# GpSimd's low halves signalled piece by piece, weights kept earlier, the second PV behind K's projection, and a split wait for the first scores, in a banded attention and FFN kernel

## The chip, the core and the metric

The kernel runs on one core of one Trainium2 chip. The metric is the device time of one execution in microseconds. The kernel before took 2201.57 us (median of 3 runs, 2192.87 to 2208.58 us).

## What is computed

For 8 batches of 1024 rows by 512, the reference computes a layer norm, 16 heads of attention in which scores outside a band of 64 columns to either side are set to 0 (and still count in the softmax), and a small network of 64 units with 16 hidden values each. Input, attention and network are added:

```python
xn = layernorm(x)
Q, K, V = (xn @ W + b for (W, b) in ((Wq, bq), (Wk, bk), (Wv, bv)))    # 16 heads of 64
columns = where(band, Q @ K.T, 0.0)
out = softmax(columns) @ V @ Wo + bo
s = xn @ Win + bin_
g = sum(relu(s[..., None] * W1 + b1) * W2) + b2
return x + out + (g @ Wout + bout)
```

## The kernel before

**Steps.** Two heads make a pair, so there are 8 pairs in each of 8 batches, and the program of each engine is one call of `run_steps` (L187) that issues 66 steps. Step n has k = n modulo 8. It projects Q, K and V for pair n (`project`, L1133, matmuls on L1143), it attends for pair j = n - 1 (scores, softmax), and it weighs the values (`weigh_values`, L1188, matmuls on L1199) and projects the output (`project_out`, L1149, L1158) for pair o = n - 2. The network's parts are hung into certain steps: k = 0 its input, k = 1 to 4 the 16 hidden values (on DVE L906), k = 5 its split and the next batch's statistics, k = 6 and 7 its output (L1180). The order of work on each engine is written out by hand in its `step` function, and the engines meet through counted semaphores.

**Split numbers.** Each factor is held as a high and a low half, and a product is three passes of matmuls: hi*hi, hi*lo, lo*hi. So each tile has a high half that ACT writes (a rounding copy) and a low half that DVE or GpSimd (POOL) writes as the difference.

**Softmax of pair j.** PE writes scores of two 128-row tiles and both heads per call (`scores(tp)`, tp 0 to 3, L1121, 12 matmul pairs). DVE scales and masks them into `probs` and takes the row maxima (`mask_scores`, L842 to L861), ACT exponentiates (L532), DVE makes the denominators of one half of the rows in four small instructions (`denominators(half)`: L866 `row_l`, L869, L871, L873 `neg_e`), POOL normalises eight 128x256 tiles of that half (`normalise_weights`, L388, each instruction increments `normed`), ACT rounds four of them into `p_hi` (L588), and POOL writes the low half of four tiles, `p_lo` (`weights_low(half, h)`, L399 to L403). In a step POOL runs output_low(0), normalise(0), low(0,0), output_low(1), normalise(1), low(0,1), low(1,0), low(1,1). Of the four instructions of one `weights_low` only the last increments the semaphore `p_lo`:

```python
for t in tiles_of(half):
    last = pool.tensor_tensor(p_split[lo][:, h, t], probs[:, h, t], p_split[hi][:, h, t], ALU.subtract)
last.then_inc(p_lo, 1)
```

SyncE (SP) then transposes the weights by DMA, one DMA for each half, head and part (`transpose_weights`, L240 to L247), and PE's `weigh_values(half)` waits for the four transposes of its half. In the text PV(0) and PV(1) are its two calls in a step.

**Values.** V's projection goes through ACT (`value_lines`, L559 to L571) into `vT`. DVE sums three partial sums into a mean in small instructions (`centre_values`: L935, L937, L939 on 128x1, then L941 subtracts it from `vT`), PE transposes `vT` at the end of the step (`transpose_values`, L1182, L1186), ACT and DVE split it, and DVE makes `v_back` (L1051, 128x1). The first DVE work of the next step is `mask_scores(0)`.

**Scores and their inputs.** ACT (L580) and DVE (`qk_low`, L930) split Q and K by halves of 512 rows, in the order Q first half, K first half, Q second half, K second half; the counter `qk_lo` rises by one for each, so by four in a step. `scores(0)`, the first work of PE in a step, waits for all four of the step before.

**Weights.** In the first 8 steps (`split`) the raw weights of pair n + 1 are split by ACT (`split_high`, L475) and DVE (L794) into the single buffer `w_split`; before ACT may overwrite it, the split of pair n must have been stored to the internal tensor `w_kept` (`keep_weights`, L217 to L219). SP issues these stores between the transposes of the step, each followed by a load of the raw weights of pair n + 2. All later steps load the kept weights (`load_kept`, L221).

Of the kernel before, what the change touches and what calls it, by code (L numbers as in the profile page):

```python
# [15 lines left out]
def band_attention_ffn(nc, x, Wq, bq, Wk, bk, Wv, bv, Wo, bo, Win, bin_, W1, b1, W2, b2, Wout, bout, out):  # L16
# [16 lines left out]
    with ExitStack() as ctx:  # L33
# [148 lines left out]
        def tiles_of(half):  # L182
            return range(4 * half, 4 * half + 4)
# [29 lines left out]
        def _(sp):  # L213
# [26 lines left out]
            def transpose_weights(j, half, h, part):  # L240
                u = 2 * half + h
                if 2 * j - 1 + half > 0:
                    sp.wait_ge(pv_done, 2 * j - 1 + half)
                sp.wait_ge((p_hi, p_lo)[part], 4 * j + u + 1)
                sp.dma_start_transpose(pT[half][h][part][:],
                                       p_split[part][:, h, 4 * half:4 * half + 4].rearrange("p t w -> p (t w)")) \
                    .then_inc(pT_in[half], 16)  # L247
# [35 lines left out]
            def step(n, b, k, proj=True, attend=True, out_proj=True, split=False, split_next=False, last=False):  # L283
                j = n - 1
                next_pair = (k + 1) % PAIRS
                loads_next = proj and not (last and k == PAIRS - 1)

                def next_weights(i):
                    if split:
                        keep_weights(n, i, k)  # L290
                        if k < PAIRS - 2:
                            load_raw(i, k + 2)
                    elif loads_next:
                        load_kept(n, i, next_pair)

                def first_kept(i):
                    sp.wait_ge(w_got[i], 16 * (n + 1))
                    load_kept(n, i, 0)

                if 2 <= n <= PAIRS + 1:  # L300
                    keep_output(n - 1, n - 2)
                elif out_proj:
                    load_output_kept(n - 1, (k - 2) % PAIRS)
                if split and k > 0:
                    load_output_raw(k)
                if k == 2 and b > 0:
                    store(b - 1, 1)
                if k in (2, 3) and not last:
                    load_x(b + 1, k - 2)
                if attend:  # L310
                    transpose_weights(j, 0, 0, hi)
                    transpose_weights(j, 0, 0, lo)
                    transpose_weights(j, 0, 1, hi)
                if k == 1 and b > 0 and proj:
                    store(b - 1, 0)
                if proj:
                    next_weights(V_)
                if attend:
                    transpose_weights(j, 1, 0, hi)
                    transpose_weights(j, 0, 1, lo)  # L320
                if proj:
                    next_weights(Q_)
                if attend:
                    transpose_weights(j, 1, 1, hi)
                if proj:
                    next_weights(K_)
                if n == PAIRS - 1:
                    first_kept(V_)
                    first_kept(Q_)
                if attend:  # L330
                    transpose_weights(j, 1, 0, lo)
                    transpose_weights(j, 1, 1, lo)
                if n == PAIRS - 1:
                    first_kept(K_)
# [12 lines left out]
        def _(pool):  # L347
# [31 lines left out]
            def step(n, b, k, proj=True, attend=True, out_proj=True, last=False, **_):  # L379
# [17 lines left out]

                def weights_low(half, h):
                    pool.wait_ge(p_hi, 4 * j + 2 * half + h + 1)  # L399
                    for t in tiles_of(half):  # L400
                        last = pool.tensor_tensor(p_split[lo][:, h, t], probs[:, h, t], p_split[hi][:, h, t],  # L401
                                                  ALU.subtract)
                    last.then_inc(p_lo, 1)  # L403

                def add_biases(p):

# [299 lines left out]
        def _(dve):  # L706
# [132 lines left out]
            def step(n, b, k, proj=True, attend=True, out_proj=True, split_next=False, last=False, **_):  # L839
                j, o = n - 1, n - 2  # L840

                def mask_scores(tp):  # L842
                    if n == 1 and tp == 0:
                        dve.wait_ge(mask_set, 1)
                    if j > 0 and tp % 2 == 0:
                        dve.wait_ge(p_lo, 4 * j - 2 + tp)
                    if j < PAIRS and tp == 0:
                        dve.wait_ge(unit_s_ready, 2 * j + 2)
                    dve.wait_ge(scored, 4 * j + tp + 1)
                    for h in range(2):  # L850
                        for i in range(2):
                            c, t = column(tp, h, i), 2 * tp + i

                            dve.tensor_tensor_reduce(out=probs[:, h, t],  # L854
                                                     in0=ps[SCORE_BANK[tp][h]][:, i * WIN:i * WIN + WIN],
                                                     in1=mask[:], scale=unit_s[:, j % PAIRS:j % PAIRS + 1],
                                                     scalar=0.0, op0=ALU.mult, op1=ALU.max,
                                                     accum_out=row_max[:, c:c + 1]).then_inc(masked, 1)
                    dve.wait_ge(masked, 16 * j + 4 * tp + 4)
                    cols = slice(4 * tp, 4 * tp + 4)  # L860
                    dve.tensor_scalar(neg_max[:, cols], row_max[:, cols], -1.0, None, ALU.mult).then_inc(max_ready, 1)  # L861
# [206 lines left out]
        def _(pe):  # L1068
# [48 lines left out]
            def step(n, b, k, proj=True, attend=True, out_proj=True, split=False, last=False, **_):  # L1117
# [2 lines left out]

                def scores(tp):  # L1121
                    if tp == 0:
                        pe.wait_ge(qk_lo, 4 * j + 4)
                    for i in range(2):
                        t = 2 * tp + i
                        for a, (qp, kp) in enumerate(PASSES):
                            for h in range(2):
                                rows = slice(h * D, h * D + D)
                                last = pe.matmul(ps[SCORE_BANK[tp][h]][:, i * WIN:i * WIN + WIN],  # L1129
                                                 qT[qp][rows, t * P:t * P + P], kT[kp][rows, t * P:t * P + WIN],  # L1130
                                                 start=(a == 0), stop=(a == 2))
                    last.then_inc(scored, 1)
# [85 lines left out]

                if attend:
                    earlier_outputs_added(5)  # L1220
                    scores(0)
                    scores(1)
                if out_proj:
# [9 lines left out]
                if attend:  # L1233
                    masks_read(0)
                    earlier_outputs_added(7)
                    scores(2)
                    scores(3)
                if out_proj:
                    if attend:
                        masks_read(1)  # L1240
                    else:
                        pe.wait_ge(o_summed, 2 * o)
                    weigh_values(1)
                if proj:
                    if attend:
                        masks_read(1)
                    project_qk(1)
                if proj and k == 0:
                    if attend:
                        masks_read(2)  # L1250
# [164 lines left out]
```

## Time and profile before

| | us |
|---|---|
| median of 3 runs | 2201.57 |
| lowest, highest | 2192.87, 2208.58 |
| the profiled execution | 2183.65 |
| its span, first to last instruction | 2181.9 |

Engines are PE (matmul), PEld (its weight loads), DVE, ACT, POOL and SP (queue). Busy time of an engine counts executing instructions, including the time that an instruction takes longer because something holds it up inside. "Idle before" in brackets names how long the engine had nothing and which instruction released it. PEclk is the granted clock of TensorE as a share of full speed, with two levels, 1.0 (2.4 GHz) and 0.5 (1.2 GHz).

### The profile page before, as it was taken

How to read it: one execution, taken by the hardware profiler on the slowest of the kernel's cores; microseconds unless marked ns; L12 is line 12 of the kernel's file. 1: busy time of each engine (PE TensorE's matmuls, PEld its weight loads, DVE VectorE, ACT ScalarE, POOL GpSimd, SP SyncE). 2: the span in 40 equal slices, each digit the busy share in tenths (PEclk: the TensorE clock that was granted, in tenths of full speed). 3: DMA queues.
4: the chain of work that ended last, by engine and by line, in shares of the span. 5: the costliest groups of instructions: out<-in, count | busy, mean ns of one | idle time of the engine just before them, and what ended most of it. 6: DMA issues, size and time to landing. Idle time of an engine off the chain costs nothing.

```text
span 2181.9 us, 42699 instructions
## 1 busy us (share of the span) xinstructions
PE 1958.2 (90%) x14211; PEld 1107.1 (51%) x14211; DVE 1824.1 (84%) x4579; ACT 1480.3 (68%) x3961; POOL 1517.1 (70%) x2272
## 2 busy tenths in 40 slices
PE   8768799998999989998899998998989998999985
PEld 4435455554555545554455554554555554555543
DVE  7779687898789887998889888889888898888775
ACT  5767667775767756766667775775757775777753
POOL 3655657877588757867578775686748876687764
PEclk8988899999999999999999999999999999999997
DMA  4454453755366543754356654375444755365534
GB/s 124 118 134 98 97 116 84 174 112 112 69 128 160 101 93 83 164 123 99 81 103 150 136 101 102 80 186 107 87 93 103 173 102 108 78 141 112 117 78 106
DMA packets 610427, 247.04 MB, mean 113 GB/s; under 512 B 547336, under 2 KB 559648, under 8 KB 610208
## 3 DMA queue, kind: packets, MB, share of 16 engines
q1 hardware_dynamic: 610160, 244.30, 50.9%
q8 instruction: 114, 1.87, 0.4%
q14 instruction: 105, 0.86, 0.1%
q10 hardware_dynamic: 48, 0.01, 0.0%
HBM read 84.84 MB, written 25.17 MB: 50 GB/s over the span
## 4 chain that ended last, share of the span: by engine, by line
PE 34%; DVE 26%; POOL 15%; ACT 13%; issue 7%; DMA 5%; SPq 1%; DVEq 0%; ACTq 0%; POOLq 0%
PE ps L1143 17%; POOL probs L388 8%; ACT probs L532 7%; POOL p_lo L401 6%; DVE acc L888 5%; PE ps L1199 5%; PE ps L1158 4%; DVE probs L854 4%; PE ps L1129 4%; DVE v_mean L935 3%; DMA pT_lo<-p_lo 3%; DVE row_l L866 3%; DVE xn L906 2%; ACT p_hi L588 2%; DMA w_kept<-w_split 1%
## 5 line engine op out<-in xcount | busy, mean ns | idle before, releaser
L1143 PE MATMUL ps<-xT_hi,w_split 128*128 128x512 f16 x3072 | 976.8, 382 | 7.9 <-issue 4.4
L388 POOL TENSOR_SCALAR probs<-probs,inv_l,neg_e 128x256 f32<-128x256 f32 x1024 | 589.9, 592 | 283.0 <-DVE neg_e L873 281.5
L401 POOL TENSOR_TENSOR p_lo<-probs,p_hi 128x256 f16<-128x256 f32 x1024 | 678.2, 697 | 39.9 <-ACT p_hi L588 39.9
L1143 PE MATMUL ps<-xT_lo,w_split 128*128 128x512 f16 x1536 | 587.0, 382 | 0.0
L532 ACT ACTIVATE probs<-probs,neg_max 128x256 f32<-128x256 f32 x1024 | 505.7, 498 | 24.4 <-DVE neg_max L861 24.2
L1143 PEld LDWEIGHTS ps<-xT_hi,w_split 128*128 128x128 f16 x3072 | 301.8, 98 | 380.0 <-issue 26.0
L854 DVE CUSTOM_DVE_ANT_0 probs<-ps,mask,unit_s 128x256 f32<-128x256 f32 x1024 | 433.2, 478 | 44.1 <-PE ps L1129 43.6
L888 DVE SCALAR_TENSOR_TENSOR acc<-ps,unit_o,acc 128x512 f32<-128x512 f32 x512 | 356.4, 740 | 30.4 <-PE ps L1158 30.4
L395 POOL TENSOR_TENSOR oT_lo<-o_sum,oT_hi 128x512 f16<-128x512 f32 x128 | 149.0, 1164 | 311.4 <-ACT o_sum L600 311.4
L1158 PE MATMUL ps<-wo_split,oT_hi 128*128 128x512 f16 x1024 | 317.9, 393 | 17.2 <-DVE xT_lo L743 9.2
L588 ACT ACTIVATE p_hi<-probs 128x1024 f16<-128x1024 f32 x256 | 269.5, 1053 | 83.1 <-POOL probs L388 82.8
L1199 PE MATMUL ps<-pT_hi,v 128*64 128x256 f16 (+1 forms) x2560 | 201.8, 260 | 47.5 <-DMA pT_lo<-p_lo 38.8
L1143 PEld LDWEIGHTS ps<-xT_lo,w_split 128*128 128x128 f16 x1536 | 151.1, 98 | 161.4 <-issue 3.3
L1129 PE MATMUL ps<-kT_hi,qT_hi 64*128 64x256 f32 x1024 | 164.7, 310 | 54.5 <-DVE kT_lo L930 46.9
L596 ACT ACTIVATE oT_hi<-ps,v_back 128x512 f16<-128x512 f32 x128 | 86.7, 677 | 168.7 <-PE ps L1199 168.7
L1158 PE MATMUL ps<-wo_split,oT_lo 128*128 128x512 f16 x512 | 200.7, 392 | 0.0
L532 ACT ACTIVATION_READ_ACCUMULATOR probs<-probs,neg_max 128x1 f32 x1024 | 195.5, 191 | 0.0
L866 DVE SCALAR_TENSOR_TENSOR row_l<-e,row_sum 128x8 f32<-128x8 f32 x128 | 98.6, 770 | 99.4 <-ACT e L535 99.3
L1199 PEld LDWEIGHTS ps<-pT_hi,v 128*64 128x64 f16 x2560 | 142.2, 113 | 68.5 <-issue 28.6
L1199 PE MATMUL ps<-pT_lo,v 128*64 128x256 f16 (+1 forms) x1280 | 170.2, 258 | 0.0
L1158 PEld LDWEIGHTS ps<-wo_split,oT_hi 128*128 128x128 f16 x1024 | 101.3, 101 | 130.4 <-issue 14.2
L1129 PEld LDWEIGHTS ps<-kT_hi,qT_hi 64*128 64x128 f32 x1024 | 104.2, 191 | 113.0 <-issue 72.9
(119 smaller groups left out, 2981.4 us busy)
## 6 DMA issues: line engine op xcount, KB each, us to landing
w_split<-w_kept SPq DMA_DIRECT2D x168, 256.0 KB, 3.1
acc<-in_L_attn_x SPq DMA_DIRECT2D x14, 1024.0 KB, 6.4
out_x<-acc SPq DMA_DIRECT2D x14, 1024.0 KB, 5.6
wo_split<-wo_kept SPq DMA_DIRECT2D x56, 256.0 KB, 2.9
w_kept<-w_split SPq DMA_DIRECT2D x24, 256.0 KB, 2.4
pT_hi<-p_hi SPq DMA_TRANSPOSE x256, 3.1
pT_lo<-p_lo SPq DMA_TRANSPOSE x256, 3.3
acc<-in_L_attn_x SPq DMA_DIRECT2D x4, 512.0 KB, 5.7
```

Source lines behind the costliest of these rows:

```text
L388: pool.tensor_scalar(probs[:, h, t], probs[:, h, t], inv_l[:, c:c + 1], neg_e[:, c:c + 1], ALU.mult, ALU.add).then_inc(normed, 1)
L395: pool.tensor_tensor(oT[lo][:, cols], o_sum[half][:], oT[hi][:, cols], ALU.subtract) \
L401: last = pool.tensor_tensor(p_split[lo][:, h, t], probs[:, h, t], p_split[hi][:, h, t], ALU.subtract)
L532: act.activation(probs[:, h, t], probs[:, h, t], ACT.Exp, bias=neg_max[:, c:c + 1], accum_out=row_sum[:, c:c + 1])
L588: act.activation(p_split[hi][:, h, tiles], probs[:, h, tiles], ACT.Copy).then_inc(p_hi, 1)
L854: dve.tensor_tensor_reduce(out=probs[:, h, t], in0=ps[SCORE_BANK[tp][h]][:, i * WIN:i * WIN + WIN], in1=mask[:], scale=unit_s[:, j % PAIRS ...
L866: dve.scalar_tensor_tensor(row_l[:, cols], e0[:, cols], float(N - WIN), row_sum[:, cols], ALU.mult, ALU.add).then_inc(l_ready, 1)
L888: dve.scalar_tensor_tensor(acc[:, parity, t], ps[OUT_BANK[t]][:], unit_o[:, pair % PAIRS:pair % PAIRS + 1], acc[:, parity, t], ALU.mult, A ...
L1129: last = pe.matmul(ps[SCORE_BANK[tp][h]][:, i * WIN:i * WIN + WIN], qT[qp][rows, t * P:t * P + P], kT[kp][rows, t * P:t * P + WIN], start= ...
L1143: last = pe.matmul(dst[:], w[wp][:, i, c], xT[xp][:, c, half * LINE:half * LINE + LINE], start=(c == 0 and a == 0), stop=(c == KC - 1 and ...
L1158: last = pe.matmul(ps[OUT_BANK[t]][:], oT[op][:, t * P:t * P + P], wo[wp][:], start=(a == 0), stop=(a == 2))
L1199: last = pe.matmul(ps[PV_BANK[half]][h * D:h * D + D, q0:q0 + (end - first) * P], v[:, o % 2, (4 * half + c) % T, h, vp], pT[half][h][pp][ ...
```

## The change

Four edits:

- POOL's `weights_low` increments `p_lo` after each of its four instructions, and each instruction first waits until the one before has completed. The counters that SP and DVE wait for are scaled from 4 to 16 in a step, so they wait for the same instructions as before.
- SP, in the first 8 steps, stores the three split weights (and loads the raw ones of pair n + 2) at the beginning of the step, ahead of the other DMAs of the step.
- PE runs the projection of K's first half before PV(1), not behind it.
- `scores(0)` waits for two of the four halves of Q and K, `scores(1)` for all four. In step 1 a wait for V's ACT copies is added ahead of `scores(0)`.

```diff
-                sp.wait_ge((p_hi, p_lo)[part], 4 * j + u + 1)
+                sp.wait_ge(*((p_hi, 4 * j + u + 1), (p_lo, 16 * j + 4 * u + 4))[part])
...
                 def next_weights(i):
-                    if split:
+                    if not split and loads_next:
+                        load_kept(n, i, next_pair)
+
+                def first_kept(i):
+                    sp.wait_ge(w_got[i], 16 * (n + 1))
+                    load_kept(n, i, 0)
+
+                if split:
+                    for i in (V_, Q_, K_):
                         keep_weights(n, i, k)
                         if k < PAIRS - 2:
                             load_raw(i, k + 2)
-                    elif loads_next:
-                        load_kept(n, i, next_pair)
...
                     pool.wait_ge(p_hi, 4 * j + 2 * half + h + 1)
-                    for t in tiles_of(half):
-                        last = pool.tensor_tensor(p_split[lo][:, h, t], probs[:, h, t], p_split[hi][:, h, t],
-                                                  ALU.subtract)
-                    last.then_inc(p_lo, 1)
+                    for i, t in enumerate(tiles_of(half)):
+                        if 16 * j + 8 * half + 4 * h + i > 0:
+                            pool.wait_ge(p_lo, 16 * j + 8 * half + 4 * h + i)
+                        pool.tensor_tensor(p_split[lo][:, h, t], probs[:, h, t], p_split[hi][:, h, t],
+                                           ALU.subtract).then_inc(p_lo, 1)
...
-                        dve.wait_ge(p_lo, 4 * j - 2 + tp)
+                        dve.wait_ge(p_lo, 16 * j - 8 + 4 * tp)
...
                     if tp == 0:
+                        pe.wait_ge(qk_lo, 4 * j + 2)
+                    if tp == 1:
                         pe.wait_ge(qk_lo, 4 * j + 4)
...
                     earlier_outputs_added(5)
+                    if n == 1:
+                        pe.wait_ge(v_in, 2)
                     scores(0)
                     scores(1)
...
+                if proj:
+                    if attend:
+                        masks_read(1)
+                    project_qk(1)
                 if out_proj:
                     if attend:
                         masks_read(1)
                     else:
                         pe.wait_ge(o_summed, 2 * o)
                     weigh_values(1)
-                if proj:
-                    if attend:
-                        masks_read(1)
-                    project_qk(1)
```

On POOL, one `weights_low` and what follows it in the middle of a step, before:

```order
L401 TENSOR_TENSOR p_lo<-probs,p_hi 128x256 [waits p_hi]
L401 TENSOR_TENSOR p_lo<-probs,p_hi 128x256 x3
L395 TENSOR_TENSOR oT_lo<-o_sum,oT_hi 128x512 [waits o_summed,oT_hi]
L388 TENSOR_SCALAR probs<-probs,inv_l,neg_e 128x256 [waits norm_ready]
L388 TENSOR_SCALAR probs<-probs,inv_l,neg_e 128x256 x7
```

and in the changed kernel, whose lines are numbered anew:

```order
L404 TENSOR_TENSOR p_lo<-probs,p_hi 128x256 [waits p_lo,p_hi]
L404 TENSOR_TENSOR p_lo<-probs,p_hi 128x256 [waits p_lo] x3
L396 TENSOR_TENSOR oT_lo<-o_sum,oT_hi 128x512 [waits o_summed,oT_hi]
L389 TENSOR_SCALAR probs<-probs,inv_l,neg_e 128x256 [waits norm_ready]
L389 TENSOR_SCALAR probs<-probs,inv_l,neg_e 128x256 x7
```

No instruction moved; each of the four now waits for the one ahead of it.

On SP, step 4 of the first batch from its beginning, before (`w_lo_v`, `w_lo_q`, `w_lo_k` are raised when DVE has finished the low half of that weight):

```order
L233 DMA wo_kept<-wo_split 128x1024 [waits wo_lo]
L229 DMA wo_raw<-in_L_attn_Wo 128x512 [waits wo_lo]
L245 DMA_TRANSPOSE pT_hi<-p_hi 128x8x128 [waits p_hi,pv_done]
L245 DMA_TRANSPOSE pT_lo<-p_lo 128x8x128 [waits p_lo,pv_done]
L245 DMA_TRANSPOSE pT_hi<-p_hi 128x8x128 [waits p_hi,pv_done]
L219 DMA w_kept<-w_split 128x1024 [waits w_lo_v]
L215 DMA w_raw<-in_L_attn_Wv 128x4x128
L245 DMA_TRANSPOSE pT_hi<-p_hi 128x8x128 [waits p_hi,pv_done]
L245 DMA_TRANSPOSE pT_lo<-p_lo 128x8x128 [waits p_lo,pv_done]
L219 DMA w_kept<-w_split 128x1024 [waits w_lo_q]
L215 DMA w_raw<-in_L_attn_Wq 128x4x128
L245 DMA_TRANSPOSE pT_hi<-p_hi 128x8x128 [waits p_hi,pv_done]
```

and now:

```order
L219 DMA w_kept<-w_split 128x1024 [waits w_lo_v]
L215 DMA w_raw<-in_L_attn_Wv 128x4x128
L219 DMA w_kept<-w_split 128x1024 [waits w_lo_q]
L215 DMA w_raw<-in_L_attn_Wq 128x4x128
L219 DMA w_kept<-w_split 128x1024 [waits w_lo_k]
L215 DMA w_raw<-in_L_attn_Wk 128x4x128
L233 DMA wo_kept<-wo_split 128x1024 [waits wo_lo]
L229 DMA wo_raw<-in_L_attn_Wo 128x512 [waits wo_lo]
L245 DMA_TRANSPOSE pT_hi<-p_hi 128x8x128 [waits p_hi,pv_done]
L245 DMA_TRANSPOSE pT_lo<-p_lo 128x8x128 [waits p_lo,pv_done]
```

All three stores, and three loads of raw weights, now stand ahead of the transposes.

On PE, behind `scores(3)` of a later step, before: the end of PV(1) and the projection of K that follows:

```order
L1199 MATMUL ps<-pT_hi,v 64x128 x2
L1199 MATMUL ps<-pT_lo,v 64x128 x2
L1199 MATMUL ps<-pT_hi,v 64x128 x2
L1143 MATMUL ps<-xT_hi,w_split 128x512 [waits w_got_k,masked]
L1143 MATMUL ps<-xT_lo,w_split 128x512
L1143 MATMUL ps<-xT_hi,w_split 128x512 x2
```

and now, the end of the projection of K and PV(1) behind it:

```order
L1147 MATMUL ps<-xT_lo,w_split 128x512
L1147 MATMUL ps<-xT_hi,w_split 128x512
L1203 MATMUL ps<-pT_hi,v 64x128 [waits pT_in_1,masked]
L1203 MATMUL ps<-pT_hi,v 64x128
L1203 MATMUL ps<-pT_lo,v 64x128 x2
```

The wait for the transposed weights of the second half (`pT_in_1`) moved behind 12 matmuls of K.

## Rows read from the trace of the kernel before

**Rows 1.** The page: span; busy time of each engine.

```profile
span 2181.9 us, 42699 instructions
PE 1958.2 (90%) x14211; PEld 1107.1 (51%) x14211; DVE 1824.1 (84%) x4579; ACT 1480.3 (68%) x3961; POOL 1517.1 (70%) x2272
```

**Rows 2.** Waits: engine, line waited for, us in total, times, longest.

```profile
PE ps L1129 <- DVE kT_lo L930: 46.9, 18, 11.3
PE ps L1186 <- DVE acc L920: 42.0, 8, 6.2
PE ps L1186 <- DVE vT L941: 24.6, 8, 4.8
PE ps L1199 <- DMA pT_lo<-p_lo: 38.8, 30, 4.9
ACT w_split L475 <- DMA w_kept<-w_split: 67.3, 18, 6.9
```

**Rows 3.** PE in order of time, from 1029 us (start, us, what, [idle before]).

```profile
1029.57 1.04 PE L1186 MATMUL ps<-ident,vT 128*128 128x128 f32 x8
...
1060.41 0.39 PE L1143 MATMUL ps<-xT_hi,w_split 128*128 128x512 f16 x1
...
1062.80 0.38 PE L1143 MATMUL ps<-xT_hi,w_split 128*128 128x512 f16 x1
1069.37 1.94 PE L1186 MATMUL ps<-ident,vT 128*128 128x128 f32 x8 [6.19 <-DVE acc L920]
```

**Rows 4.** DVE and POOL in order of time, from 1057 us.

```profile
1057.86 7.02 DVE L935 TENSOR_TENSOR v_mean<-v_sums 128x1 f32<-128x1 f32 x1
1067.94 1.28 DVE L920 TENSOR_TENSOR acc<-ps,acc 128x512 f32<-128x512 f32 x2
1057.29 7.58 POOL L401 TENSOR_TENSOR p_lo<-probs,p_hi 128x256 f16<-128x256 f32 x12
```

**Rows 5.** DVE by line: count | busy us, mean ns | idle before; L935's min/median/max ns.

```profile
L866 DVE SCALAR_TENSOR_TENSOR row_l<-e,row_sum 128x8 f32<-128x8 f32 x128 | 98.6, 770 | 99.4 <-ACT e L535 99.3
L935 DVE TENSOR_TENSOR v_mean<-v_sums 128x1 f32<-128x1 f32 x64 | 93.8, 1466 | 3.4 <-ACT vT L570 3.4
L1051 DVE TENSOR_TENSOR v_back<-v_new,bias_scaled 128x1 f32<-128x1 f32 x64 | 57.3, 896 | 0.0
L935 DVE TENSOR_TENSOR v_mean<-v_sums x64: 144/375/7018, 38.0 to 2124.2; 128x1 f32<-128x1 f32 x64
```

**Rows 6.** POOL and DVE in order of time, 22 to 40 us.

```profile
22.51 0.45 POOL L370 TENSOR_SCALAR_AFFINE_SELECT mask<-mask 128x256 f32<-128x256 f32 x1
23.03 0.47 POOL L373 TENSOR_SCALAR_AFFINE_SELECT mask<-mask 128x256 f32<-128x256 f32 x1
30.57 9.82 POOL L409 TENSOR_TENSOR acc<-acc,bias_row 128x512 f32<-128x512 f32 x8
38.00 1.17 DVE L935 TENSOR_TENSOR v_mean<-v_sums 128x1 f32<-128x1 f32 x1 [3.45 <-ACT vT L570]
```

**Rows 7.** ACT and PE in order of time, 150 to 242 us.

```profile
150.19 0.72 ACT L475 ACTIVATE w_split<-w_raw,w_scale 128x512 f16<-128x512 f32 x1 [5.13 <-DMA w_kept<-w_split]
161.94 0.58 PE L1129 MATMUL ps<-kT_hi,qT_hi 64*128 64x256 f32 x2 [8.87 <-DVE kT_lo L930]
...
241.08 0.58 PE L1129 MATMUL ps<-kT_hi,qT_hi 64*128 64x256 f32 x2 [8.28 <-DVE kT_lo L930]
```

**Rows 8.** Windows: stretch, us, busy (x) of PE, PEld, DVE, ACT, POOL, PEclk, DMA share, GB/s.

```profile
47.29:320.11 272.82, 216.32 (x1467) 122.63 (x1468) 216.78 (x560) 185.17 (x492) 158.42 (x244) 0.88 0.46 107
582.76:841.31 258.55, 238.99 (x1769) 135.07 (x1768) 224.57 (x558) 179.90 (x483) 189.03 (x281) 0.99 0.52 115
1004.00:1032.00 28.00, 28.00 (x214) 15.85 (x216) 23.76 (x76) 20.30 (x57) 19.37 (x29) 1.00 0.43 84
```

**Rows 9.** POOL and PE in order of time, 1028 to 1035 us.

```profile
1028.50 7.60 POOL L401 TENSOR_TENSOR p_lo<-probs,p_hi 128x256 f16<-128x256 f32 x12
1034.39 0.25 PE L1199 MATMUL ps<-pT_hi,v 128*64 128x128 f16 x2 [0.87 <-DMA pT_lo<-p_lo]
```

More of the change, by code:

```diff
@@ L288, in next_weights @@
                 def next_weights(i):
-                    if split:
-                        keep_weights(n, i, k)
-                        if k < PAIRS - 2:
-                            load_raw(i, k + 2)
-                    elif loads_next:
+                    if not split and loads_next:
                         load_kept(n, i, next_pair)
@@ L298, in first_kept @@
                     load_kept(n, i, 0)
+                if split:
+                    for i in (V_, Q_, K_):
+                        keep_weights(n, i, k)
+                        if k < PAIRS - 2:
+                            load_raw(i, k + 2)
                 if 2 <= n <= PAIRS + 1:
```

## Prediction

> **What bounds the kernel now.** I read the page's busy times first [rows 1]: PE is busy 1958.2 of 2181.9 us, so it is the bound, and at most 223.7 us of idle can be won, plus what a lower clock costs it. DVE is busy 84%, but that number has to be doubted below. The second view was the chain of waits, to see what PE's idle time waits for [rows 2]. Three things carry it: the transposes of V wait for DVE (42.0 + 24.6 = 66.6 us, 16 times), the first scores of a step for the second half of K (46.9 us, 18 times), and the weighing of values for the last transpose DMA (38.8 us, 30 times). Then I went to the timeline at the longest of the first kind. PE stands still for 6.19 us before L1186 [rows 3]. DVE released it, and DVE was late because one 128x1 addition, L935, took 7.02 us, from 1057.86 to 1064.88; that is to within 0.01 us where POOL's uninterrupted run of twelve p_lo pieces ends, 1057.29 + 7.58 = 1064.87 [rows 4]. The same line takes 144 ns at its fastest [rows 5]. So DVE's load is partly false: small instructions with SBUF inputs are held for the rest of a run on POOL. Last, a clean stretch: from 1004 to 1032 us PE is busy 28.00 of 28.00 us at clock 1.00 [rows 8]. That is what a plain step costs when nothing waits, against 258.55 / 8 = 32.3 us a step in one of the later batches [rows 8], with its network steps, which hold more matmuls.
>
> **Piece by piece on POOL: what it takes away.** The excess of three DVE lines alone is 98.6 - 128 x 0.17 = 77 us (L866), 93.8 - 64 x 0.15 = 84 us (L935) and 57.3 - 64 x 0.15 = 48 us (L1051) [rows 5], with L935's minimum of 0.15, and 0.17 as an estimate from it for eight columns. Does a boundary between pieces let DVE in? The nearest rows are POOL's eight bias additions, two-input instructions of which each signals: 30.57 to 40.39 us, 1.23 us apart. Within them L935 starts at 38.00 and takes 1.17 [rows 6]: it is let in at the next boundary, and is over 1.2 us before the run is. With pieces of 7.60 / 12 = 0.63 us [rows 9] I expect at most 0.7 us instead of up to 7.0. In the stretch of rows 4 v_mean then ends near 1058.5, 6.4 us earlier; the addition on L920 that released PE comes 4.3 us behind it (1069.22 less 1064.88), so at 1062.8, while PE finishes at 1063.2. The gap closes. Over the 16 such gaps I count 60 of 66.6 us.
>
> Behind such a gap TensorE's granted clock is at its lower level: the eight transposes take 1.94 us, and 1.04 in the step before, where nothing stood still [rows 3]. It lasts into the next step; I put twice that difference, 1.8 us, on each of 14 gaps: 25 us. The v_back addition (L1051) stands just ahead of the first masking of a step, and its 48 us of excess delay what PE waits for there only where DVE has no slack; I count a sixth, 8 us.
>
> **What it costs.** A piece that waits for the one ahead loses the overlap. The nearest rows are the two mask instructions, of which the second waits for the first: 22.51 + 0.45 = 22.96, next start 23.03, so 0.07 us of gap [rows 6], where p_lo pieces stand 0.63 us apart today, from 7.60 for 12 [rows 9], and overlap (that by 0.04 us is an estimate). That is 0.11 us a piece, 1024 x 0.11 = 113 us more of POOL's time, which is 70% busy [rows 1], so not a bound by load. It is one by latency: the eight pieces low(0,0) and low(0,1) lie ahead of PV(0), and PV(0) already waits for their transpose, as by 0.87 us at 1034.39, when the twelve pieces began at 1028.50 [rows 9]. 8 x 0.11 = 0.9 us on that path. Against it stands that `neg_e` comes earlier where L866 was held, so that normalise(1) starts earlier. I let half of the 56 later steps pay: 28 x 0.9 = 25 us. Both ends: nothing where the earlier start hides it, 64 x (0.9 + 0.3 for DVE instructions let in) = 77 us if every step pays. I take 25 since 30 waits of this kind in 64 steps are seen today [rows 2]. The last two steps, with nothing else to do, pay 12 x 0.11 twice: -3 us.
>
> A rule of the Trainium skill speaks against all of this gain (SBUF — State Buffer, section "Who interferes with whom"): DVE with two SBUF inputs and GpSimd with SBUF reads share a port pair, and the one that comes second is blocked until the first one's instruction has finished. By that, a hold would end at the next piece today, after 0.63 us at most, and more boundaries would bring nothing. The trace disagrees: 7.02 us across twelve pieces [rows 4]. It is one of the rivals below.
>
> **Weights kept at the beginning of the step.** In the first batch ACT waits 67.3 us, 18 times, for the store of the weights that it is to overwrite [rows 2], 5.13 us of it at one call in step 3, and since ACT takes its work in order, K's second half is late: PE stands 8.87 us at 161.94 [rows 7]. The stores wait on SP behind transposes that themselves wait for POOL. Issued first, a store has half a step before ACT asks for it. The cost: keep of K waits for the low half from the end of the step before, which DVE makes just before the values are split; behind it on SP stand the transposes of this step, which need `probs` normalised and so are due much later. Three such large gaps, 8.87 and 8.28 us [rows 7] and the longest, 11.3 us [rows 2], make 28 us; I count all of them. The first batch also runs at clock 0.88: its 1467 matmuls take 216.3 us, where at the later rate they would take 1467 x 238.99 / 1769 = 198 [rows 8]: 18 us, of which 14 are counted here (the rest is in the 25 above). Bounds: 0 if another wait of ACT takes the place, 60 us if the stretch comes to the later steps' pace.
>
> **Scores(0) on two halves.** The other 46.9 - 28.4 = 18.5 us of waits for K's second half are short ones, (46.9 - 28.4) / 15 = 1.2 us on average. scores(0) can now run in each, 12 matmul pairs; DVE is earlier as well. I count 10 us. Nothing is given up.
>
> **PV(1) behind K.** A projection of one half is 12 matmuls: in rows 3 one lasts from 1060.41 to 1063.18, 2.8 us. The mean wait for the transposes is 38.8 / 30 = 1.3 us [rows 2]. PV(1) needs the transpose issued last; I put a quarter of the 38.8 us [rows 2] on it, 10 us, an estimate, since PV(0) stands in front of it and takes most of the waiting. It is gone, and the 12 x 0.11 = 1.3 us by which low(1,1) comes later, fit under 2.8 as well. ACT reads PV(1) only behind its fourth call of exponentials, whose scores PE wrote just before, so the delay of PV(1) is hidden; if it were not, 1.5 us of each step (what is left of 2.8 behind the wait) would be the price, 96 us in 64 steps. But PE wants the result only in project_out(4), behind both projections of V and half the output. I take 10 us gained.
>
> **Sum.** 60 + 25 + 8 + 28 + 14 + 10 + 10 = 155 us gained, 28 us paid, 127 net. 2183.65 - 127 = 2057 us for an execution like the profiled one. The median of the runs lies 2201.57 / 2183.65 = 1.008 above it, so 2073; I say 2070 us.
>
> **Rivals.** (A) *POOL takes over, partly.* All steps pay the whole 77 us in front of PV(0). For it: the clean steps have no room there, 30 waits already. Against: the earlier neg_e. 2183.65 - 155 + 77 + 3 = 2109, as a median 2126 us. (B) *A boundary frees nothing on POOL,* the page's per-instruction lock, or one that only sees the engine as free for too short a time. Only the edits on SP and PE remain: 28 + 14 + 10 + 10 = 62, less 28: 2150, as a median 2167 us. Against: rows 6. (C) *Slower: the self-wait is dear.* POOL's completion signal costs more than in rows 6, for instance 0.45 us a piece; then 8 pieces in 64 steps are 230 us in front of PV(0), and 2183.65 - 155 + 230 = 2259, as a median 2277 us. It decides from 155 / (64 x 8) = 0.30 us a piece. For it: the mask rows are one case, without DVE interfering. Against: 0.07 us is a measured gap.
>
> **How the numbers follow.** The forecast gets 0.68, (A) 0.18, (B) 0.07, (C) 0.07. About 1% is what a measurement of this kernel can tell from no change. The forecast, (A) and most of (B) are faster by over 1%: 0.91. Within 1%: 0.04, from (B) and the foot of (C). Slower: 0.05. The range reaches from 2020 (both POOL costs hidden, 28 us, and some of the remaining 20 us of PV(0) waits gone) to 2130, which takes in (A).
>
> **What would show it.** L935's longest near 0.7 us, and L866 and L1051 with means under 0.4; DVE's busy time down by about 200 us though no work left it. No gap before the V transposes above 1 us, and the clock near 1.00 from 320 us on. ACT's waits for w_kept near 0, the first batch some 45 us shorter. p_lo pieces 0.74 us apart. Waits of PE for pT_lo stay near 30 us, all before PV(0). Wrong if L935 still shows several us; if pT_lo waits exceed 80 us; or if pieces are over 0.9 us apart.

## The result, and the profile after

The changed kernel takes 2048.05 us (median of 4 runs, 2046.27 to 2049.84); the kernel before, beside it, 2205.07 us (4 runs, 2192.87 to 2215.52). The ratio is 0.929 (95% interval 0.9239 to 0.934): faster by 7%. The forecast was 2070 us, a ratio of 0.940. Here and below medians are of all runs, while ratios leave out the runs that were over 1.5% above the fastest of the same kernel.

The page of the changed kernel: span, busy times, and by line the shares of the chain that ended last.

```profile
span 2044.5 us, 42955 instructions
PE 1931.4 (94%) x14211; PEld 1086.5 (53%) x14211; DVE 1636.9 (80%) x4579; ACT 1482.7 (73%) x3961; POOL 1576.1 (77%) x2272
...
POOL probs L389 20%; POOL p_lo L404 17%; PE ps L1147 14%; PE ps L1203 5%; PE ps L1162 4%; DMA pT_lo<-p_lo 3%; PE ps L1133 3%; POOL oT_lo L396 3%; POOL acc L411 3%; ACT probs L534 2%; PE ps L1184 1%; ACT oT_hi L598 1%; PE ps L1073 1%; PE ps L1190 1%; ACT o_sum L602 1%
```

With the same instructions, DVE is busy 187 us less than in [rows 1], PE 27 us less, and POOL 59 us more. The span is 137.4 us shorter: 110.6 us of PE's idle time (223.7 less 113.1) and 26.8 us of its busy time, for the same matmuls at a mean granted clock of 0.981, before 0.961. The chain now runs through POOL's normalising and p_lo.

Waits of PE in the changed kernel (us in total, times, longest), against [rows 2]:

```profile
PE ps L1203 <- DMA pT_lo<-p_lo: 55.2, 39, 6.2
...
PE ps L1133 <- DVE kT_lo L932: 5.5, 4, 4.4
...
PE ps L1190 <- DVE acc L922: 1.9, 1, 1.9
```

The V transposes (L1190, before L1186) waited 66.6 us for DVE (on `acc` and `vT`) and now 1.9; the first scores 46.9 and now 5.5. Of PE's large waits only that for the transposed weights grew, from 38.8 to 55.2 us. ACT's wait for `w_kept`, 67.3 us before, is no longer among the waits.

DVE by line, first count, busy us and mean ns, then min/median/max for the first sum of the mean, against [rows 5]:

```profile
L868 DVE SCALAR_TENSOR_TENSOR row_l<-e,row_sum 128x8 f32<-128x8 f32 x128 | 32.0, 250 | 88.0 <-ACT e L537 87.9
...
L1053 DVE TENSOR_TENSOR v_back<-v_new,bias_scaled 128x1 f32<-128x1 f32 x64 | 19.3, 302 | 0.0
...
L937 DVE TENSOR_TENSOR v_mean<-v_sums x64: 148/346/1178, 37.6 to 1990.4; 128x1 f32<-128x1 f32 x64
```

`row_l` fell from 770 to 250 ns on average, `v_back` from 896 to 302, and the longest `v_mean` from 7018 to 1178 ns (that one beside the bias additions). The place of rows 3 and 4, one network step, in order of time on POOL, DVE and PE:

```profile
977.71 9.31 POOL L404 TENSOR_TENSOR p_lo<-probs,p_hi 128x256 f16<-128x256 f32 x12
```

```profile
979.09 0.15 DVE L937 TENSOR_TENSOR v_mean<-v_sums 128x1 f32<-128x1 f32 x1
979.28 0.61 DVE L939 TENSOR_TENSOR v_mean<-v_mean,v_sums 128x1 f32<-128x1 f32 x1
```

```profile
984.09 0.38 PE L1147 MATMUL ps<-xT_hi,w_split 128*128 128x512 f16 x1
984.49 1.06 PE L1190 MATMUL ps<-ident,vT 128*128 128x128 f32 x8
```

`v_mean` is let in 1.4 us into a run of twelve pieces, and the transposes follow the projection without a gap and at full clock (1.06 us for eight, against 1.94 behind the gap in [rows 3]). The price is in the first row: twelve pieces take 9.31 us, 0.78 each, against 7.58 before (medians over all unbroken runs of twelve in the two traces: 9.74 and 8.09).

By stretches (us, busy of PE, PEld, DVE, ACT, POOL, PEclk, DMA share, GB/s), steps 1 to 7 and a later batch, against [rows 8]:

```profile
46.51:278.76 232.25, 207.58 (x1470) 117.98 (x1470) 197.84 (x561) 186.47 (x494) 174.89 (x244) 0.95 0.56 125
...
530.21:773.59 243.38, 236.38 (x1772) 132.42 (x1772) 199.21 (x558) 180.12 (x484) 194.23 (x281) 1.00 0.58 122
```

Steps 1 to 7 are 40.6 us shorter (272.8 before), the later batch 15.2 us (258.6 before), and its clock is full throughout.

### The profile page after: what moved, and what is told of

It reads as the page before. It is cut to its first block, busy times and chain, and to the rows that moved or that the text cites. A ratio compares the mean times of both kernels' runs of the same rounds, so it can differ in the third digit from the quotient of the medians.

```text
span 2044.5 us, 42955 instructions
## 1 busy us (share of the span) xinstructions
PE 1931.4 (94%) x14211; PEld 1086.5 (53%) x14211; DVE 1636.9 (80%) x4579; ACT 1482.7 (73%) x3961; POOL 1576.1 (77%) x2272
## 4 chain that ended last, share of the span: by engine, by line
POOL 44%; PE 30%; issue 13%; ACT 6%; DVE 4%; DMA 3%; POOLq 0%; SPq 0%; DVEq 0%; ACTq 0%
POOL probs L389 20%; POOL p_lo L404 17%; PE ps L1147 14%; PE ps L1203 5%; PE ps L1162 4%; DMA pT_lo<-p_lo 3%; PE ps L1133 3%; POOL oT_lo L396 3%; POOL acc L411 3%; ACT probs L534 2%; PE ps L1184 1%; ACT oT_hi L598 1%; PE ps L1073 1%; PE ps L1190 1%; ACT o_sum L602 1%
## 5 line engine op out<-in xcount | busy, mean ns | idle before, releaser
L389 POOL TENSOR_SCALAR probs<-probs,inv_l,neg_e 128x256 f32<-128x256 f32 x1024 | 604.9, 608 | 244.5 <-DVE neg_e L875 244.5
L404 POOL TENSOR_TENSOR p_lo<-probs,p_hi 128x256 f16<-128x256 f32 x1024 | 723.8, 707 | 81.9 <-ACT p_hi L590 2.9
L534 ACT ACTIVATE probs<-probs,neg_max 128x256 f32<-128x256 f32 x1024 | 505.4, 498 | 13.8 <-DVE neg_max L863 12.9
L1162 PE MATMUL ps<-wo_split,oT_hi 128*128 128x512 f16 x1024 | 306.3, 381 | 12.9 <-POOL oT_lo L396 5.3
L1203 PE MATMUL ps<-pT_hi,v 128*64 128x256 f16 (+1 forms) x2560 | 203.7, 261 | 55.6 <-DMA pT_lo<-p_lo 55.2
L1162 PE MATMUL ps<-wo_split,oT_lo 128*128 128x512 f16 x512 | 194.7, 380 | 0.0
L1133 PE MATMUL ps<-kT_hi,qT_hi 64*128 64x256 f32 x1024 | 159.6, 308 | 12.3 <-DVE acc L890 6.3
L1133 PE MATMUL ps<-kT_lo,qT_hi 64*128 64x256 f32 x1024 | 145.6, 280 | 0.0
L1133 PE MATMUL ps<-kT_hi,qT_lo 64*128 64x256 f32 x1024 | 145.3, 280 | 0.0
```

Source lines behind the costliest of these rows:

```text
L389: pool.tensor_scalar(probs[:, h, t], probs[:, h, t], inv_l[:, c:c + 1], neg_e[:, c:c + 1], ALU.mult, ALU.add).then_inc(normed, 1)
L534: act.activation(probs[:, h, t], probs[:, h, t], ACT.Exp, bias=neg_max[:, c:c + 1], accum_out=row_sum[:, c:c + 1])
L1162: last = pe.matmul(ps[OUT_BANK[t]][:], oT[op][:, t * P:t * P + P], wo[wp][:], start=(a == 0), stop=(a == 2))
L1203: last = pe.matmul(ps[PV_BANK[half]][h * D:h * D + D, q0:q0 + (end - first) * P], v[:, o % 2, (4 * half + c) % T, h, vp], pT[half][h][pp][ ...
```

## Experiments

The kernel before differs by chip and hour: 2205 us beside the changed kernel, and 2173, 2163 and 2203 us in the three groups below, while the changed kernel took 2048 and 2052. Ratios are to the kernel before in the same group; differences of microseconds are taken within a group, or across groups where said.

### First group: the parts apart, and the signal without the wait

```diff
 # e1_no_pool, from the changed kernel (the counters of SP and DVE as before, too)
-                    for i, t in enumerate(tiles_of(half)):
-                        if 16 * j + 8 * half + 4 * h + i > 0:
-                            pool.wait_ge(p_lo, 16 * j + 8 * half + 4 * h + i)
-                        pool.tensor_tensor(p_split[lo][:, h, t], ..., ALU.subtract).then_inc(p_lo, 1)
+                    for t in tiles_of(half):
+                        last = pool.tensor_tensor(p_split[lo][:, h, t], ..., ALU.subtract)
+                    last.then_inc(p_lo, 1)
```

> The changed kernel with POOL's edit alone undone (one signal and no self-waits for four p_lo pieces). If the hold on DVE's small instructions was the main loss, L935 is back at up to 7 us and the time rises to 2130 to 2160 us (0.97 of the kernel before). Rival: the edits on SP and PE brought most of the gain, and the time stays under 2080 us (0.943).

Measured: 2157.56 us, ratio 0.9921 (0.9887 to 0.9954), 106 us above the changed kernel (across groups). The hold is back, and with it the V transposes' wait:

```profile
L936 DVE TENSOR_TENSOR v_mean<-v_sums x64: 142/426/7751, 38.5 to 2095.3; 128x1 f32<-128x1 f32 x64
```

```profile
PE ps L1189 <- DVE acc L921: 46.1, 8, 6.2
...
PE ps L1189 <- DVE vT L942: 12.7, 9, 3.7
```

The three edits on SP and PE without POOL's bring 0.8%, which is less than SP's edit brings alone (e3 below).

```diff
 # e2_pool_alone, from the kernel before: the edit on POOL, with the counters of SP and DVE
 # e3_keep_alone, from the kernel before: the edit on SP
```

> The kernel before with POOL's edit alone. Hold theory: 2100 to 2125 us (0.955 to 0.965), the gaps before the V transposes gone, the first batch as long as before. Rival (SP and PE edits carry it): over 2160 us.

Measured: 2107.95 us, ratio 0.9683 (0.964 to 0.9726), so 65 us less than the kernel before; that is my 60 + 25 + 8 - 25 - 3 = 65. ACT's wait for the stores is untouched, and the wait for the transposes has grown (38.8 us and 30 times before):

```profile
ACT w_split L476 <- DMA w_kept<-w_split: 79.0, 18, 7.2
...
PE ps L1200 <- DMA pT_lo<-p_lo: 56.1, 45, 5.7
PE ps L1200 <- DVE row_max L855: 12.9, 18, 1.2
```

The last line is mostly the same wait under another name: 16 of its 18 waits end 0.135 us after a transpose has landed, as do 2 of 4 in the kernel before (2.0 us). With them PE waits 68.3 us for transposes, against 40.8: 27.5 more, where I had counted 25. The V transposes wait 5.6 us for DVE, against 66.6 (61 less, 60 counted), and PE's busy time is 23.8 us less (25 counted for the clock). So these three terms fit one by one, and not only the sum.

> The kernel before with SP's edit alone (weights kept at the beginning of a step). Forecast from the sum: 42 us less, so 2160 to 2170 us (0.98), all of it in the first batch. Rival: another wait of ACT takes the place of the removed one, under 10 us gained (over 0.995).

Measured: 2137.94 us, ratio 0.9818 (0.976 to 0.9877), 35 us less. The wait for `w_kept` is gone from ACT's waits, and the seven steps from the first scores of step 1 take 241.6 us, against 272.8 before. e1 contains this edit and is 20 us slower, by ratio 1%: while DVE was held, the edits on PE cost time. The traces show where. From step 8 to the last the first scores of e1 and e3 lie 1825 and 1804 us apart, while the seven steps ahead take 236 and 242. In e1 PE waits less for K's second half (6.1 us against 30.8), but more for DVE's sums into `acc` ahead of the scores (23.8 against 8.8) and for `xT_lo` ahead of the output (17.4 against 7.9), and it is busy 10 us longer for the same matmuls. Which of the two PE edits does it was not tried.

```diff
 # e4_signal_only, from the changed kernel
                     for i, t in enumerate(tiles_of(half)):
-                        if 16 * j + 8 * half + 4 * h + i > 0:
-                            pool.wait_ge(p_lo, 16 * j + 8 * half + 4 * h + i)
                         pool.tensor_tensor(..., ALU.subtract).then_inc(p_lo, 1)
```

> The changed kernel in which each p_lo piece signals but none waits for the one ahead. Theory S, a signal at each boundary is enough to let DVE in (as among the bias additions): L935 stays under 1.3 us, pieces 0.63 us apart, time 2030 to 2048 us (0.921 to 0.929). Theory W, it is the self-wait that lets DVE in: some DVE instructions are again held for several us and the time is near that of the kernel with POOL's edit undone, 2120 to 2160 us.

Measured: 2158.95 us, ratio 0.9919 (0.9878 to 0.996): the time of e1. Theory S has fallen, W holds. In its trace, on POOL and on DVE in order of time, a piece is again 7.57 / 12 = 0.63 us and the hold is back:

```profile
2069.01 7.57 POOL L402 TENSOR_TENSOR p_lo<-probs,p_hi 128x256 f16<-128x256 f32 x12
```

```profile
2069.59 7.02 DVE L935 TENSOR_TENSOR v_mean<-v_sums 128x1 f32<-128x1 f32 x1
```

A signal at each boundary does nothing; that POOL waits for its own completion there does all of it.

### Second group: the edits on PE, and fewer self-waits

> The changed kernel again, beside the next three on the same chip: 0.93 to 0.945 of the kernel before, the measure for the other three.

Measured: 2051.96 us, ratio 0.9477 (0.9449 to 0.9504).

```diff
 # e5_no_pvk, from the changed kernel: weigh_values(1) and its waits ahead of project_qk(1) again
```

> The changed kernel with PV(1) put back ahead of K's projection. By my sum, which gave this edit 10 us, and with the last p_lo pieces 1.3 us later than before: 10 to 25 us slower than the changed kernel (0.5% to 1.2%). Rival: PV(0) takes all the waiting and the place of PV(1) makes no difference, under 4 us.

Measured: 2064.87 us, ratio 0.9536 (0.9506 to 0.9567): 12.9 us slower, as the sum had it (10). The wait for the last transpose is back in front of PV(1); a0 has the first of these lines with 59.9 us, 42 times, and not the second:

```profile
PE ps L1203 <- DMA pT_lo<-p_lo: 63.5, 50, 5.2
PE ps L1203 <- DVE row_max L856: 13.6, 18, 1.8
```

Again 17 of the 18 waits put down to `row_max` end 0.135 us after a transpose has landed, so they are waits for it. In the profiled executions PE is idle 22.7 us longer than in a0 (139.1 against 116.4), and busy 14.7 us less (1921.8 against 1936.5), at a mean clock of 0.985 against 0.980. The edit is thus worth more in waiting than in time; what keeps the clock lower with it was not tried.

```diff
 # e6_no_sc, from the changed kernel
                     if tp == 0:
-                        pe.wait_ge(qk_lo, 4 * j + 2)
-                    if tp == 1:
                         pe.wait_ge(qk_lo, 4 * j + 4)
...
-                    if n == 1:
-                        pe.wait_ge(v_in, 2)
```

> The changed kernel in which scores(0) waits for all four halves again (and without the added wait in step 1). By my sum 10 us slower (0.5%), in short gaps before scores(0). Rival: with DVE no longer held, K's second half is always there in time, and the edit is worth under 3 us.

Measured: 2048.94 us, ratio 0.9464 (0.9441 to 0.9488): 3 us faster than the changed kernel, if anything. The wait is there,

```profile
PE ps L1131 <- DVE kT_lo L932: 18.1, 12, 5.4
```

against 5.8 us, 4 times, in a0; but the 12.3 us more of waiting don't reach the end. In the profiled executions two other waits of PE are 4.4 (for `acc`) and 3.4 us (for transposes) shorter than in a0, all its idle time is 5.5 us longer (121.9 against 116.4), and its busy time is 11.6 us shorter (1924.9 against 1936.5), at a mean clock of 0.984 against 0.980. So what the edit saves in this wait is lost in others and in the clock; why the clock differs is not shown. In its size the rival was right (under 3 us), not in its reason.

```diff
 # e7_wait_every_second, from the changed kernel
-                        if 16 * j + 8 * half + 4 * h + i > 0:
+                        if i == 2:
                             pool.wait_ge(p_lo, 16 * j + 8 * half + 4 * h + i)
```

> The changed kernel with one self-wait in each group of four p_lo pieces, ahead of the third, and a signal on each. If a drained boundary is what lets DVE in, the longest hold is now two pieces (1.3 us) and between groups up to three or four (2.6 us); POOL's run of twelve is some 1 us shorter. Theory L (POOL's latency ahead of PV(0) is what bounds the changed kernel): 5 to 15 us faster than the changed kernel. Rival H (holds still cost more than latency): 10 to 40 us slower.

Measured: 2025.98 us, ratio 0.9358 (0.9332 to 0.9384): 26 us faster than the changed kernel beside it, beyond what theory L gave. It beats both kernels. One self-wait in four pieces keeps DVE free, the run of twelve is 8.0 us instead of 9.3, and PE waits 20 us less for transposes than in a0. Of the 26 us, 14.7 are idle time of PE (116.4 to 101.7) and 11.1 are busy time, at a clock of 0.985 against 0.980. From its trace: `v_mean`, a run of twelve, the wait for the transposes, and a batch (columns as above):

```profile
L937 DVE TENSOR_TENSOR v_mean<-v_sums x64: 148/375/1347, 37.9 to 1974.2; 128x1 f32<-128x1 f32 x64
```

```profile
947.84 8.01 POOL L404 TENSOR_TENSOR p_lo<-probs,p_hi 128x256 f16<-128x256 f32 x12
```

```profile
PE ps L1203 <- DMA pT_lo<-p_lo: 39.9, 30, 6.1
```

```profile
772.53:1015.53 243.00, 236.29 (x1770) 132.50 (x1768) 197.50 (x558) 180.14 (x484) 192.57 (x281) 1.00 0.59 122
```

PE is busy 236.3 of 243.0 us in that batch.

### Third group: the price of latency, where the wait is needed, and the hold by itself

```diff
 # e8_normalise_waits, from the changed kernel
+                            if half or h or t or j:
+                                pool.wait_ge(normed, 16 * j + 8 * half + 4 * h + t % 4)
                             pool.tensor_scalar(probs[:, h, t], probs[:, h, t], inv_l[:, c:c + 1], neg_e[:, c:c + 1],
```

> The changed kernel in which each of the 16 normalise instructions of a step also waits for the one ahead. Theory L (POOL's latency in front of PV(0) bounds the changed kernel): 16 boundaries of 0.1 us, eight to sixteen of them on the path, 50 to 90 us slower than the changed kernel. Rival P (PE's own work bounds it): under 15 us slower.

Measured: 2137.38 us, ratio 0.9749 (0.9672 to 0.9826): some 85 us above the changed kernel across groups, by the ratios 3 to 5%. 16 more boundaries in a step, 64 x 16 x 0.1 = 102 us of POOL's time, cost most of their length: 55 us of waiting in front of PV, and 32.5 us of PE's busy time (1963.9 less 1931.4), at a mean granted clock of 0.963 against 0.981:

```profile
PE ps L1205 <- DMA pT_lo<-p_lo: 110.4, 46, 7.1
```

So POOL's latency is on the path of the changed kernel, as the chain says, though POOL is busy only 77%.

```diff
 # e9_wait_each_group, from the changed kernel: the self-wait once, ahead of each group of four
+                    if 4 * j + 2 * half + h > 0:
+                        pool.wait_ge(p_lo, 16 * j + 8 * half + 4 * h)
                     for t in tiles_of(half):
                         pool.tensor_tensor(..., ALU.subtract).then_inc(p_lo, 1)
```

> Signals on each piece, one self-wait ahead of each group of four. If the boundary with a self-wait is what lets DVE in, the longest hold is one group, 2.6 us, and the run of twelve costs 0.2 us more than before the change. Expected between the one with a wait ahead of each third piece and the kernel with POOL's edit undone: 2035 to 2080 us by the numbers of the last runs (0.94 to 0.96).

Measured: 2060.99 us, ratio 0.9384 (0.9284 to 0.9484; its runs spread from 2048 to 2087, and the ratio leaves the last out). That is within what was expected, but can't be told from the changed kernel, with 0.929 and 0.9477 in the other groups. The trace is of the execution of 2087 us, so only its holds are read here. The first sum of the mean is held for one group at most, but `row_l` for longer, as the group low(0,0) is followed by `output_low(1)` with no self-wait between:

```profile
L937 DVE TENSOR_TENSOR v_mean<-v_sums x64: 143/269/2765, 36.7 to 2031.2; 128x1 f32<-128x1 f32 x64
```

```profile
L868 DVE SCALAR_TENSOR_TENSOR row_l<-e,row_sum x128: 152/168/3556, 55.1 to 2054.0; 128x8 f32<-128x8 f32 x128
```

```diff
 # e10_no_wait_01, from e7_wait_every_second
-                        if i == 2:
+                        if i == 2 and (half, h) != (0, 1):
```

> One self-wait ahead of the third piece, but none in low(0,1), which lies right ahead of PV(0)'s transposes. If v_mean's hold of 2.6 us there costs PE nothing, PV(0) comes 0.1 us earlier and the time is that of the kernel with a wait ahead of every third piece, or up to 5 us less; if it costs, the V transposes show gaps and it is 5 to 30 us slower.

Measured: 2034.96 us, ratio 0.928 (0.921 to 0.935), 9 us above e7 across groups, but by the ratios 0.8% below it (0.928 against 0.9358): which of the two is faster the groups can't tell. `v_mean` is held for up to 3.34 us again, and PE waits for it (4.3 us in e7):

```profile
PE ps L1190 <- DVE acc L922: 13.9, 8, 3.9
```

Last, a kernel of its own, of which the core is

```python
for kind in KINDS:                                      # POOL: 12 instructions of one kind, with or without signals
    for fill in (160, 224, 288, 352, 416, 480):         # DVE: two PSUM additions of this width, to shift the moment
        for r in range(4):
            dve.tensor_tensor(tiny[1 + r][:], small[:, 2:3], small[:, 3:4], ALU.add).then_inc(probed, 1)
            dve.wait_ge(probed, seen)
```

> Leaves out the whole computation and writes zeros. For eight kinds of a run of twelve POOL instructions, and six delays each, DVE issues four 128x1 additions of two SBUF inputs beside the run, and their durations tell how long they are held. Theory K (the kind of instruction decides, not the signal): the first addition lasts to the end of the run in most p_lo-like runs, signalled or not, and ends at the next boundary in the bias-like and normalise-like ones; with a self-wait it always ends at the next boundary. Rival (phase decides alone): all kinds without a self-wait hold the addition to the end at some delays and let it in at others, in like proportion.

Measured, the additions beside runs like p_lo's with a signal on each piece, then with a self-wait on each, then beside 128x512 bias additions with signals (min/median/max ns):

```profile
L85 DVE TENSOR_TENSOR tiny<-small x24: 149/592/614, 52.2 to 93.9; 128x1 f32<-128x1 f32 x24
...
L85 DVE TENSOR_TENSOR tiny<-small x24: 148/160/598, 99.5 to 147.5; 128x1 f32<-128x1 f32 x24
...
L85 DVE TENSOR_TENSOR tiny<-small x25: 315/1185/1186, 244.8 to 334.9; 128x1 f32<-128x1 f32 x25
```

Both theories missed. Without a self-wait, too, every addition beside p_lo-like runs ended at the next boundary, 614 ns at the most in 24 with signals and 609 in 24 without, and none was held to the end. So neither the kind of instruction nor these six moments are enough to bring about the hold of 7 us that the full kernel shows.

The full kernel, too, shows both. In the trace of the kernel before, 37 `v_back` additions start inside a run of twelve pieces that has neither signals within a group nor self-waits: 25 end at the next boundary (695 ns at the most), and 12 are held to the end of the run (2749 ns at the least). Two of them, each with the p_lo pieces that POOL does meanwhile:

```profile
905.17 0.62 DVE L1051 TENSOR_TENSOR v_back<-v_new,bias_scaled 128x1 f32<-128x1 f32 x1
...
904.46 1.93 POOL L401 TENSOR_TENSOR p_lo<-probs,p_hi 128x256 f16<-128x256 f32 x3
```

```profile
1032.35 3.77 DVE L1051 TENSOR_TENSOR v_back<-v_new,bias_scaled 128x1 f32<-128x1 f32 x1
...
1031.65 4.45 POOL L401 TENSOR_TENSOR p_lo<-probs,p_hi 128x256 f16<-128x256 f32 x7
```

Both start beside the seventh of twelve pieces, 67 and 69 ns after its start; so the moment within a piece does not decide. What does go with the outcome is the place in the program: all 24 that the network's next instruction follows on DVE (`xn`, L906) were let in, and 12 of the 13 others were held. In e1, e3 and e4 it is 89 of 89 and 37 of 42. Whether it is this next instruction or something else in those steps was not tried, and the cause is open.

POOL in order of time (start, length, both in us), the last run of twelve with signals only and the first with self-waits:

```profile
91.33 7.56 POOL L57 TENSOR_TENSOR low<-a,h 128x256 f16<-128x256 f32 x12 [0.33 <-DVE marks L81]
99.22 8.88 POOL L57 TENSOR_TENSOR low<-a,h 128x256 f16<-128x256 f32 x12 [0.33 <-DVE marks L81]
```

The eleven boundaries cost (8.88 - 7.56) / 11 = 0.12 us each.

## Why the prediction was right, step by step

**POOL's hold on DVE** was right in size: 65 us forecast net for POOL's edit, 65 measured alone, and so were three of its terms (e2). Its three DVE lines lost 66% to 73% of their busy time, the gaps before the V transposes went from 66.6 to 1.9 us (60 were counted). DVE's busy time fell by 187 us, where about 200 were named.

**The step that failed is the reason given for it.** I read from the bias additions, which signal at each boundary, that a boundary lets DVE in [rows 6]. e4 has a signal at each boundary and holds DVE as before. What frees DVE is the self-wait, which the change also has; the bias additions let DVE in for a reason that was not found, as did every run of the small kernel. The trace of the kernel before held the counterexample: small instructions are not always held for the rest of a run, as 25 of 37 `v_back` additions were let in at the next boundary 22 of them at boundaries without a signal, and none with a self-wait. With the edit made as e4 makes it, my argument would have promised the same gain, and e4 has none of it.

**The weight of the rivals.** (B), the lock of one instruction, falls: e1 and e4 show holds of 7.75 and 7.02 us across twelve instructions, and the changed kernel gets rid of them. The rule of the Trainium skill (SBUF — State Buffer, "Who interferes with whom") describes the small kernel, where each addition ended with the instruction beside it, and in the full one those 25 of 37, but not the other 12, nor the 7.75 and 7.02 us. (C) falls by the price of a piece: 9.31 / 12 = 0.78 us apart with DVE's instructions let in, and 8.01 / 12 = 0.67 in e7, against a decision at 0.63 + 0.30. (A) was half right: POOL does take over, 44% of the chain, 85 us for another 16 boundaries in e8. But the changed kernel paid only 16 us more of waiting for transposes, and e7 gets 26 us back. The sign given for these waits, near 30 us, was missed (55.2); it stayed short of the 80 that was to refute the sum.

**Weights kept early**: 42 us forecast, 35 measured alone (31 of them in the first seven steps), and 40.6 in the length of steps 1 to 7 with all four edits. The clock part came with it, 0.88 to 0.95.

**Scores on two halves**: 10 us forecast, none found (e6, 3 us the other way). The wait was read rightly, but its removal was counted as gained time, where other waits and a lower clock took it back. This is the term that was mis-sized.

**PV(1) behind K**: 10 us forecast, 12.9 measured.

**The sum** gave 2057 us for one execution, and the profiled one took 2046.27; the median missed by 22 us (2070 to 2048.05). The parts, as measured, add: e2, e3, e5 and e6 give 65 + 35 + 12.9 - 3 = 110 us, and the whole 111 in the second group. The order matters, though: PE's two edits lost 20 us while DVE was held (e1 against e3), and gained 10 once it was free. Beside the first measurement the whole gives 157 us. That is the kernel before, whose time moves between 2163 and 2205 us, while the changed one stays within 4 us. That the held time varies from run to run would explain it; single profiles can't show that. The 127 us of the sum lie between 111 and 157, and so does the ratio (0.940; measured 0.929 and 0.9477); that the total came as close as it did is in part luck.

## What to carry to other kernels

Small instructions on one engine whose longest duration is tens of times their shortest, and ends exactly where a run on another engine ends, are not work but a hold; look at min and maximum of a line before believing a busy share. A run of POOL instructions can be opened for DVE by a wait for its own completion in the middle, where a signal alone did nothing; put as few such waits as keep the hold short, since each costs POOL's latency. And a wait that is removed is not yet time gained: look at what the engine waits for next, and at its busy time, as its clock may have moved. Where the profile names a releaser that had long been done, as `row_max` here, look for a DMA that landed just before.

## What the runs showed of the hardware

- In the full kernel a DVE instruction with SBUF inputs, 128x1, can be held up to 7.75 us, across twelve POOL instructions of two SBUF inputs, signalled or not (e1, e4). It is not always so: in the kernel before 25 of 37 `v_back` additions beside such a run ended at the next boundary. A self-wait on POOL at each boundary ends the hold within one piece, and one ahead of each third piece within 1.35 us.
- By itself, the same pair of instructions shows no such hold: 48 of 48 additions without self-waits ended by the next boundary, 614 ns at most. Whether addresses, traffic of the other engines, or what each engine did just before makes the difference was not tried.
- A self-wait at a POOL boundary costs 0.12 us in the small kernel. In the full one twelve pieces take 7.57 us without (e4) and 8.01 with three self-waits (e7), some of it DVE's own instructions let in. The medians over all unbroken runs of twelve are 8.05 us (e4), 8.43 (e7) and 9.74 (the changed kernel, a self-wait on each piece).
- PE's busy time fell by 32.8 us from the kernel before to e7 (1958.2 to 1925.4) with the same matmuls, as the mean granted clock rose from 0.961 to 0.985.
